# Fetches, buffers and slots of the sorted leaf trees in an eight-block attention and feed-forward kernel

## What is computed

```python
def _fff(x, node_w, node_b, w1, b1, w2, b2):
    xf = x.reshape(-1, D)
    cur = jnp.zeros((N,), jnp.int32)
    for _ in range(DEPTH):                       # 4 decisions
        score = jnp.einsum('nd,nd->n', xf, node_w[cur]) + node_b[cur]
        cur = 2 * cur + 1 + (score >= 0).astype(jnp.int32)
    sel = jax.nn.one_hot(cur - N_NODES, N_LEAVES)
    hidden = jax.nn.relu(jnp.einsum('nd,ldh->lnh', xf, w1) + b1[:, None, :]) * sel.T[:, :, None]
    return jnp.einsum('lnh,lho->no', hidden, w2) + sel @ b2
q, k, v = _fff(x, *q_tree), _fff(x, *k_tree), _fff(x, *v_tree)
attn = jax.nn.softmax(jnp.einsum('bqd,bkd->bqk', q, k) / np.sqrt(128), axis=-1)
x = x + jnp.einsum('bqk,bkd->bqd', attn, v)
```

## Time and profile before

| what | us |
|---|---|
| median of two runs | 1637.05 (1636.76 to 1637.35) |
| the profiled execution, whole | 1632.61 |
| its span, first to last instruction | 1630.4 |
| of it slots 34 to 61, the sparse groups | 290.6 |
| of it slots 62 to 81, attention of this block | 67.5 |
| PE busy, whole span | 1119.4 (69%) |
| DVE busy | 901.1 (55%) |
| mean granted clock of PE | 0.767 of full |

### The profile page before, as it was taken

How to read it: one execution, slowest core, us unless ns; L and a number is a source line. 1 busy time by engine, 2 the same in 40 slices (tenths; PEclk the granted TensorE clock), 3 DMA queues, 4 the chain that set the end, 5 groups by cost and what they waited for, 6 DMA issues and landing times. The chain is left out here.

```text
span 1630.4 us, 21584 instructions
## 1 busy us (share of the span) xinstructions
PE 1119.4 (69%) x6345; PEld 824.8 (51%) x6347; DVE 901.1 (55%) x3102; ACT 547.1 (34%) x1095; POOL 408.6 (25%) x467
## 2 busy tenths in 40 slices
PE   4788799999676542439268858954464459758862
PEld 2656598999544442127146555543343337525631
DVE  7677656666488866713477746421121115645768
ACT  3475344444322220113146513311011115436641
POOL 1343000000011000433754305720034005124411
PEclk9899799999855555659569958965565559968985
DMA  6342100000040203022243101222233222024301
GB/s 228 103 119 64 27 1 1 2 0 1 12 144 0 72 26 103 27 83 82 68 127 103 48 1 46 91 70 66 68 107 99 67 67 57 16 60 113 108 6 51
DMA packets 110301, 103.37 MB, mean 63 GB/s; under 512 B 11184, under 2 KB 89392, under 8 KB 109808
## 3 DMA queue, kind: packets, MB, share of 16 engines
q1 hardware_dynamic: 102768, 87.26, 18.9%
q0 software_dynamic: 7424, 14.83, 3.0%
HBM read 62.07 MB, written 40.37 MB: 63 GB/s over the span
## 5 line engine op out<-in xcount | busy, mean ns | idle before, releaser
L850 DVE TENSOR_REDUCE mha_nm<-mha_pS 128x16 f32<-128x1024 f32 x96 | 117.2, 1220 | 24.5 <-PE mha_pS L612 24.5
L790 POOL TENSOR_TENSOR mha_ks<-KS,w_ctx 104x1024 fp32r<-104x1024 f32 (+1 forms) x48 | 90.9, 1895 | 119.7 <-POOLq L100 79.0
L2167 PE MATMUL tree_pZ<-w_ctx,tree_xs 128*128 128x128 f32 x96 | 24.9, 409 | 134.9 <-DMA tree_xs<-leaf_rows 134.7
L2462 DVE COPY tree_xsT<-tree_pZ 128x512 f32<-128x512 f32 x24 | 16.6, 691 | 172.6 <-PE tree_pZ L2167 172.6
L2284 ACT ACTIVATE tree_hid<-tree_pZ,tree_leaf 64x128 f32<-64x128 f32 x96 | 27.0, 356 | 248.0 <-PE tree_pZ L2175 248.0
L1443 ACT ACTIVATE ffn_hid<-ffn_pH,w_ffn 128x512 f32<-128x512 f32 x128 | 85.4, 688 | 54.3 <-PE ffn_pH L1366 53.7
L733 ACT ACTIVATE XH<-mha_pST 128x1024 f32<-128x1024 f32 x96 | 97.8, 1019 | 10.9 <-PE mha_pST L633 10.8
L612 PE MATMUL mha_pS<-mha_ks,mha_qs 96*128 96x256 f32 (+1 forms) x384 | 80.8, 338 | 25.8 <-DVE mha_nm L850 18.9
L1379 PEld LDWEIGHTS ffn_pE<-W2R,ffn_hid 128*128 128x128 f32 x768 | 94.1, 193 | 4.3
L1379 PE MATMUL ffn_pE<-W2R,ffn_hid 128*128 128x128 f32 x768 | 94.6, 277 | 0.0
L1555 DVE SCALAR_TENSOR_TENSOR ffn_acc<-ffn_pE,ffn_wt,ffn_acc 128x128 f32<-128x128 f32 x192 | 54.0, 343 | 65.0 <-PE ffn_pE L1379 65.0
(11 more groups left out here) (519 smaller groups left out, 2981.8 us busy)
## 6 DMA issues: line engine op xcount, KB each, us to landing
mha_qs<-queries SPq DMA_DIRECT2D x72, 256.0 KB, 4.0
tree_leaf<-in_leaves_dram SPq DMA_DIRECT2D x96, 96.5 KB, 2.0
queries<-mha_qh SPq DMA_DIRECT2D x24, 256.0 KB, 2.1
queries<-mha_ql SPq DMA_DIRECT2D x24, 256.0 KB, 2.4
leaf_rows<-top_none SPq DMA_DIRECT2D x12, 512.0 KB, 6.7
tree_xs<-leaf_rows SPq DMA_DIRECT2D x24, 256.0 KB, 3.0
leaf_results<-tree_ys SPq DMA_DIRECT2D x24, 256.0 KB, 2.3
EW<-in_L_W_dram SPq DMA_DIRECT2D x32, 128.0 KB, 2.8
```

Source lines behind the costliest of these rows:

```text
L790: pool.tensor_tensor(ks[b % KB][0:K1, :, :, :], kb, hb, ALU.mult).then_inc(s["k"], 1)
L850: dve.tensor_reduce(nm[:, t, :], pS[:], AX.X, ALU.max, negate=True).then_inc(s["nm"], 1)
```

## The change

Weights get five buffers (`LB`) and rows four (`RB`). `load` is parted into `weights` and `rows`, which SP issues four and three groups ahead of the store beside them, in one run through both trees. The slots are laid out anew: 28 dense steps alone, then the 24 groups in slots 28 to 51 without a break between the trees, with a dense step beside every one of them; slot 52 has no dense step, and attention starts in slot 53, in which the last `down` still stands. The last 12 dense steps lie beside attention as before. The number of instructions of each kind stays the same.

```diff
+LB, RB = 5, 4
 class TreeSlots:
-    ALONE, SPAN = 34, XG + 2
-    K0, V0 = ALONE, ALONE + SPAN
-    S0 = V0 + SPAN
+    ALONE = 28
+    K0, V0 = ALONE, ALONE + XG
+    S0 = V0 + XG + 1
...
-        dense = list(range(self.ALONE))
-        dense += [self.K0 + n for n in range(self.SPAN) if n % 2 == 0]
-        dense += [self.V0 + n for n in range(self.SPAN) if n % 4 != 3]
+        dense = list(range(self.S0 - 1))
         dense += [self.S0 + n for n in range(NG * NCH - len(dense))]
...
-        leaf = [st.sb(f"leaf{v}", [P, GT, LEAFC]) for v in range(3)]
-        xs = [st.sb(f"xs{v}", [P, GT, P]) for v in range(3)]
+        leaf = [st.sb(f"leaf{v}", [P, GT, LEAFC]) for v in range(LB)]
+        xs = [st.sb(f"xs{v}", [P, GT, P]) for v in range(RB)]
...
-            def load(i):
+            def weights(i):
                 n, j0 = i // XG, GT * (i % XG)
                 if j0 == 0:
                     sp.wait_ge(s["table"], n + 1)
-                need(sp, s["dn"], i - 2)
+                need(sp, s["dn"], i - LB + 1)
                 for j in range(GT):
                     of = sp.value_load(...)
-                    sp.dma_start(leaf[i % 3][:, j, :], ...).then_inc(s_leaf[i % 3], 16)
+                    sp.dma_start(leaf[i % LB][:, j, :], ...).then_inc(s_leaf[i % LB], 16)
+
+            def rows(i):
+                n, j0 = i // XG, GT * (i % XG)
                 if j0 == 0:
                     sp.wait_ge(s_sent[n], 16 * T)
-                sp.dma_start(xs[i % 3][:], ...).then_inc(s_rows[i % 3], 16)
+                need(sp, s["tr"], i - RB + 1)
+                sp.dma_start(xs[i % RB][:], ...).then_inc(s_rows[i % RB], 16)
...
-            for n in range(2):
-                for i in range(XG * n, XG * n + XG + 2):
-                    if i < XG * n + XG:
-                        load(i)
-                    if i >= XG * n + 2:
-                        store(i - 2)
+            for i in range(LB - 1):
+                weights(i)
+            for i in range(RB - 1):
+                rows(i)
+            for i in range(2 * XG):
+                if i + LB - 1 < 2 * XG:
+                    weights(i + LB - 1)
+                if i + RB - 1 < 2 * XG:
+                    rows(i + RB - 1)
+                store(i)
```

More of the change, by code:

```diff
@@ L2094, in attention_trees @@
         s = {n: st.sem(n) for n in names}
-        s_leaf, s_rows = [st.sem(f"leaf_loaded{v}") for v in range(3)], [st.sem(f"rows_loaded{v}") for v in range(3)]
+        s_leaf, s_rows = [st.sem(f"leaf_loaded{v}") for v in range(LB)], [st.sem(f"rows_loaded{v}") for v in range(RB)]
         s_out = [st.sem(f"leaf_stored{u}") for u in range(2)]
@@ L2161, in rows_T @@
             def rows_T(i):
-                pe.wait_ge(s_rows[i % 3], 16 * (i // 3 + 1))
+                pe.wait_ge(s_rows[i % RB], 16 * (i // RB + 1))
                 if i == 0:
@@ L2166, in rows_T @@
                 for j in range(GT):
-                    ins = pe.transpose(pA[:, cols_of(j)], xs[i % 3][:, j, :], ident)
+                    ins = pe.transpose(pA[:, cols_of(j)], xs[i % RB][:, j, :], ident)
                 ins.then_inc(s["tr"], 1)
             def up(i):
-                pe.wait_ge(s_leaf[i % 3], 16 * GT * (i // 3 + 1))
+                pe.wait_ge(s_leaf[i % LB], 16 * GT * (i // LB + 1))
                 pe.wait_ge(s["xsT"], i + 1)
@@ L2174, in up @@
                 for j in range(GT):
-                    ins = pe.matmul(pU[0:LW, cols_of(j)], leaf[i % 3][:, j, 0:LW], xsT[i % 2][:, cols_of(j)], start=True, stop=True)
+                    ins = pe.matmul(pU[0:LW, cols_of(j)], leaf[i % LB][:, j, 0:LW], xsT[i % 2][:, cols_of(j)], start=True, stop=True)
                 ins.then_inc(s["up"], 1)
@@ L2183, in down @@
                 for j in range(GT):
-                    ins = pe.matmul(pD[:, cols_of(j)], hid[i % 2][:, cols_of(j)], leaf[i % 3][0:LW + 1, j, LW + 1:LEAFC], start=True, stop=True)
+                    ins = pe.matmul(pD[:, cols_of(j)], hid[i % 2][:, cols_of(j)], leaf[i % LB][0:LW + 1, j, LW + 1:LEAFC], start=True, stop=True)
                 ins.then_inc(s["dn"], 1)
@@ L2284, in leaf_hidden @@
                     ins = act.activation(hid[i % 2][0:LW, cols_of(j)], pU[0:LW, cols_of(j)], ACT.Relu,
-                                         bias=leaf[i % 3][0:LW, j, LW:LW + 1])
+                                         bias=leaf[i % LB][0:LW, j, LW:LW + 1])
                 ins.then_inc(s["hid"], 1)
@@ L2366, in load @@
                     sp.wait_ge(s["table"], n + 1)
-                need(sp, s["dn"], i - 2)
+                need(sp, s["dn"], i - LB + 1)
                 for j in range(GT):
                     of = sp.value_load(table[0:1, NJ * n + j0 + j:NJ * n + j0 + j + 1], min_val=0, max_val=NLEAF - 1)
-                    sp.dma_start(leaf[i % 3][:, j, :], core.A["leaves"][n, bass.ds(of, 1), :, :].rearrange("o p c -> p (o c)")).then_inc(s_leaf[i % 3], 16)
+                    sp.dma_start(leaf[i % LB][:, j, :], core.A["leaves"][n, bass.ds(of, 1), :, :].rearrange("o p c -> p (o c)")).then_inc(s_leaf[i % LB], 16)
+            def rows(i):
+                n, j0 = i // XG, GT * (i % XG)
                 if j0 == 0:
                     sp.wait_ge(s_sent[n], 16 * T)
-                sp.dma_start(xs[i % 3][:], core.tx[n][P * j0:P * j0 + GT_P, :].rearrange("(t p) d -> p t d", p=P)).then_inc(s_rows[i % 3], 16)
+                need(sp, s["tr"], i - RB + 1)
+                sp.dma_start(xs[i % RB][:], core.tx[n][P * j0:P * j0 + GT_P, :].rearrange("(t p) d -> p t d", p=P)).then_inc(s_rows[i % RB], 16)
             def store(i):
```

## The result

The changed kernel takes 1477.45 us, the median of two runs (1475.88 to 1479.03), against 1637.05 before: a ratio of 0.9025, with a 95% interval from 0.8983 to 0.9067. The forecast was 1469, from 1455 to 1500.

The account below looks back on a forecast made before the run. The sparse stretch was taken as bound by a 13.51 us round per slot from store to row fetch to next store; spread over two slots, 290.6 + 11.8 - 133.0 = 169.4, taken as 168, gives 1469 us, range 1455 to 1500.

Parts of the forecast that it names:

- The bound: Sparse stretch: PE waits for rows, held by a round of store, weights, rows and group, 13.51 us, one per slot.
- The start: Dense steps ahead of the sparse stretch: six fewer stand alone, so the stretch starts 11.8 us earlier.
- The first groups: Slots 28 to 32: `ys(0)` ends at 10.74 us and `rows_T(4)` follows at 18.6, counted from slot 28.
- The round at full clock: Sparse slots after the change: a round of 11.37 us lies over two slots, 5.69 a slot.
- the clock: PE in the sparse stretch: enters at 1.00 and keeps it, with waits of 2.4 us once and about 1.2 a slot.
- its allowance: Sparse stretch: 1.4 us taken off the gain for landings of 3.0 and three closing matmuls of a dense group.
- The half-clock rival: Sparse stretch at half clock, 8.6 us a slot: 1543 throughout, 1506 half the time; chance 0.14 for part or all.
- The signs: Changed profile: stores 5.3 to 6 us apart, row waits 25 in all, clock near 1.00, stretch 133, attention as before.
- SP's floor: SP's issue per sparse slot: loads 4.91 us plus store 0.38, together 5.3, between the round's 5.69 and PE's 4.47.
- The sum: Whole kernel: 290.6 + 11.8 - 133.0 = 169.4 us less, taken as 168, from 1637.05 to 1469.
- The gathers: k and v gathers before attention: k covered, v taken at nothing, 3 us at most; `attend` wants V at 14.7.
- The rival that ends slower: Row transfers sharing the DMA engines: landings of 20 us or more make the kernel slower, 1670 and above; chance 0.02.

Follow-up runs that it names:

- rows ahead of the weights: Against the changed kernel, SP issues the 256 KB of rows ahead of the four weights behind each store; 1465.29 us, 0.897 of before.
- the second profile: The changed kernel itself run again, nothing changed, on one chip with three other runs; 1480.10 us, 0.905 of before.
- the fillers: Against the changed kernel, four matmuls with unused results between hidden and `rows_T` in each slot with a group; 1472.18 us, 0.901 of before.
- five row buffers: Against the changed kernel, five row and four weight buffers instead of four and five, rows fetched one group further ahead; 1458.71 us, 0.893 of before.

## Why the prediction was right, and where it was off

**The bound** was read rightly. The round of store, weights, rows and group is what the kernel waited on: with the round left at one slot the new layout gives 0.998, with the layout left and the round over two slots the time is 0.914.

**The start.** Six dense steps for 11.8: 12.1, counted from the cast that ends the sorting. **The first groups**: the fifth `rows_T` was forecast 18.6 after the start of slot 28. That start was at 1051.89, the row is at 1070.79, so 18.9.

**The round at full clock.** 5.69 a slot was the forecast, 5.63 what the four slots to 1093.31 took. It lasted for these four slots.

**The step that was mis-sized** is the clock. "A stretch keeps the level it comes in with, and so I take 1.00" held over 14 slots for waits of 0.8 to 2.2 us (rows ahead of the weights) and, with one exception, not for those of 2.3 to 3.2 us; at 1.57 to 2.17 it went both ways. The forecast spread the slack evenly, "about 1.2 a slot". But a round over two slots fixes only the length of the pair. In the first profile one late fetch (5.31 behind its store, landing after 3.52) puts more of the slack into one slot and the clock falls there; in the second it fell at the fifth group, after a wait of 2.92 where the forecast itself had 2.4. Once fallen, `rows_T`, `up` and `down` take longer, the round grows from 11.4 up to 13.6, and the slack of the pair lies in one slot. The stretch came to 146.1 and 153.1, where the sum had 133.0, or 134.4 with its allowance.

The half-clock rival was sized for a PE without a pause at 8.6 a slot. Single slots were like that: 8.57 at a clock of 0.52 in the first profile (1113.14 to 1121.71). None stayed so; the clock came back within a slot or two, and the lasting price was half of 13.6, 6.8 a slot, as in the second profile.

The Trainium skill's page "TensorE: Matmul & The Clock Gate", section "HAM oscillation — how this bites in real kernels", which the prediction cites, tells of a kernel whose wait for each transfer is longer than the compute between the waits, and which starts every burst at half clock. The trace agrees in kind, in every second slot of the last part of the second profile, although the waits there, 2.7 to 3.2 us, are shorter than the some 10 us between them.

The price, from the runs: of the 12 to 19 us by which the two stretches exceed the sum, the fillers, which kept the clock up, took back 6 to 12, in spite of the work that they added. What of the rest is due to late fetches and what to the fillers' own time was not told apart.

**The signs.** PE's wait of 24.0 is the 25 forecast, but by luck: in the slots at half clock PE worked through what would have been waits. The clock (0.89 against "near 1.00") and the stretch (146.1 against 133) say that the case was another.

**SP's floor** was put at 5.3; back to back it is 5.6 to 5.7 (five row buffers). A store that SP issues right behind the rows takes 0.51, not 0.38, and the weights 3.8 or more where 3.65 was read. So two of the three floors lay closer than forecast, 5.6 to 5.7 for SP as for the round, with 4.4 for PE, and an end of the round alone could not bring 1456 with the rows first.

**The sum.** 168 was forecast, the medians give 159.6. The two profiled spans differ by 153.6: 12.1 from the start, 144.5 from the stretch, less the 3.1 of code ahead. The medians add 6.0, as that of before lies 4.4 above its profiled execution and that of after 1.6 below. So the time lies 8.5 above the forecast's 1469, where the stretch alone missed by 11.7, and part of that nearness is chance.

**The gathers** at nothing: the first `attend` came 14.7 after slot 53 began (1211.63 against 1196.94), the number forecast, with no wait for V. **Attention** behind it kept its length. **Transfers**: rows landed in 3.0 as before in the first profile and in 3.3 in the second, in the median. The rival that ends slower found no hold.

## What to carry to other kernels

Where stores and loads share one issuing queue, a store that waits for the result holds back the fetch behind it; write the round down (store, what is issued ahead of the fetch, landing, compute to the next store), and count over how many steps the buffers spread it, for the pace is the one over the other. When the round has been spread, look at what the queue takes to issue a step's transfers: here fetching the rows one group further ahead gave 21 us, and moving rows and stores to an engine with idle time 43 in all, down to PE's own pace. A round over two steps does not share its slack evenly, so price the case in which one step gets all of it, the clock included.

## What the runs showed of the hardware

PE kept full clock over 14 slots with a wait for rows of 0.8 to 2.2 us in each (rows ahead of the weights). In the two profiles of the changed kernel it lost the clock after every wait of 2.3 to 3.2 us but one of 2.59, and in other runs also after single waits of 1.57, 1.73 and 1.82, shorter than some that passed without a fall; it was granted again within a slot or two. The length of the wait alone does not tell a fall. Filling the waits with matmuls that compute nothing kept the clock at 1.00 and made the kernel faster, not slower. 256 KB of rows landed in 3.0 to 3.3 us (medians) in the kernels that moved 143 to 173 GB/s in the stretch, and in 4.4 where 206 GB/s were moved and ACT issued them. And the cast that ends the sorting, ahead of all edits, lay between 985.2 and 991.2 us in these profiles: up to 6 us between two runs come from code that nobody changed.
